# Order of SyncE's transfers, conv2 groups and row-tile waits in a two-stage convolution kernel

## What is computed

```python
x = x + L0(gn(x))      # 3x3 depthwise convolution, then three 32x32 channel mixes
x = x + L1(gn(x))      # deformable 3x3 convolution
# L1, for the normalized input v:
off = conv3x3(v, w_off)                  # 64 channels: a row and a column offset per pixel
r, c = clip(off + grid, 0, 127)
mapped = bilinear sample of v at (r, c)
return conv3x3(mapped, w_conv) + b_conv
```

## Time and profile before

| what | us |
|---|---|
| median of 3 runs | 734.21 (733.68 to 735.55) |
| the profiled execution | 738.19 |
| span of its instructions | 736.3 |
| PE busy | 655.6 (89%) |
| DVE busy | 528.4 (72%) |
| POOL busy | 478.8 (65%) |
| ACT busy | 451.1 (61%) |
| DMA engines, queue of SyncE | 57.6% of 16 engines' time |

### The profile page before, as it was taken

The page is one execution under the profiler, slowest core; times in us unless marked ns, Lnnn a source line. Parts: engine busy times, 40 slices in busy tenths (PEclk is TensorE's granted clock), DMA queues, the critical chain, the costliest instruction groups (busy, mean ns, idle before and its releaser), DMA issues.

```text
span 736.3 us, 16859 instructions
## 1 busy us (share of the span) xinstructions
PE 655.6 (89%) x6572; PEld 297.2 (40%) x6572; DVE 528.4 (72%) x1027; ACT 451.1 (61%) x778; POOL 478.8 (65%) x412
## 2 busy tenths in 40 slices
PE   4799877888996999889997999989997999789965
PEld 4334433344442444434442444433443444344422
DVE  3686987558894688828886488848987386567872
ACT  7236757676754766556665766548656666576740
POOL 4013746969687476857768376876768476977650
PEclk9999999989998999989998999999999999989989
DMA  8958723589348894498747894498945623457555
GB/s 143 186 112 152 117 59 75 137 165 160 75 105 192 176 171 115 120 210 164 141 107 168 179 201 103 106 208 174 154 114 140 145 60 77 106 126 184 128 125 130
DMA packets 135413, 101.40 MB, mean 138 GB/s; under 512 B 13696, under 2 KB 112544, under 8 KB 135328
## 3 DMA queue, kind: packets, MB, share of 16 engines
q1 hardware_dynamic: 111296, 88.47, 57.6%
q10 hardware_dynamic: 24032, 11.78, 9.6%
HBM read 31.59 MB, written 16.78 MB: 66 GB/s over the span
## 4 chain that ended last, share of the span: by engine, by line
PE 39%; SPq 21%; ACT 7%; DVE 6%; issue 5%; POOL 5%; DMA 2%; ACTq 1%; DVEq 0%; POOLq 0%
PE off_ps L816 21%; SPq L429 11%; PE c_ps L698 9%; PE off_ps L698 7%; SPq L500 7%; DMA out_dram<-x1a 2%; DVE other_row L1426 2%; ACT off_abs L1010 2%; SPq L461 1%; ACT down_ps L1008 1%; ACT beyond L1020 1%; ACT other_row L997 1%; SPq L464 1%; DVE xb L1504 1%; POOL other_col L1231 1%
## 5 line engine op out<-in xcount | busy, mean ns | idle before, releaser
L816 PE MATMUL off_ps<-x1a,wo 32*64 32x512 f32 x4608 | 289.2, 611 | 22.6 <-ACT x1a L965 12.4
L816 PEld LDWEIGHTS off_ps<-x1a,wo 32*64 32x64 f32 x4608 | 162.1, 133 | 149.8 <-issue 65.7
L1426 DVE COPY_PREDICATED other_row<-down_ps,row_diff 128x768 f32<-128x768 int32 x128 | 124.6, 1027 | 117.5 <-ACT down_ps L1008 117.5
L997 ACT ACTIVATE other_row<-row_diff 128x768 f32<-128x768 f32 x128 | 101.1, 839 | 57.9 <-POOL row_diff L1207 26.3
L1223 POOL TENSOR_TENSOR other_row<-other_row,x_strips 128x512 f32<-128x512 f32 x48 | 57.2, 1192 | 118.2 <-DVE other_row L1440 118.2
L1224 POOL TENSOR_TENSOR other_col<-other_col,other_row 128x512 f32<-128x512 f32 x64 | 87.8, 1372 | 43.6 <-DVE other_row L1440 43.6
L1008 ACT ACTIVATE down_ps<-off_ps,bias_o 128x512 f32<-128x512 f32 x64 | 42.0, 655 | 100.3 <-PE off_ps L816 85.9
L698 PE MATMUL off_ps<-xb,w 128*64 128x512 f32 x198 | 90.3, 605 | 8.2 <-DVE xb L1504 7.0
L698 PE MATMUL c_ps<-xb,w 128*64 128x512 f32 x138 | 74.5, 682 | 22.0 <-ACT x1a L965 22.0
L700 PE MATMUL off_ps<-xa,w 128*64 128x512 f32 x198 | 90.3, 605 | 0.0
L1231 POOL TENSOR_TENSOR other_col<-other_col,off_abs 128x512 f32<-128x512 f32 x64 | 82.8, 1294 | 5.0
(11 more groups left out here) (160 smaller groups left out, 1059.9 us busy)
## 6 DMA issues: line engine op xcount, KB each, us to landing
mapa<-mapped SPq DMA_DIRECT2D x224, 65.0 KB, 2.1
mapb<-mapa SPq DMA_DIRECT2D x28, 520.0 KB, 6.4
out_dram<-x1a SPq DMA_DIRECT2D x49, 256.0 KB, 4.7
xb<-in_x_dram SPq DMA_DIRECT2D x48, 256.0 KB, 10.6
xa<-in_x_dram ACTq DMA_DIRECT2D x40, 256.0 KB, 7.4
x_strips<-x1a SPq DMA_DIRECT2D x112, 81.2 KB, 2.1
x_strips<-x1a SPq DMA_DIRECT2D x112, 65.0 KB, 2.0
xa<-in_x_dram SPq DMA_DIRECT2D x16, 256.0 KB, 6.5
```

The costliest lines, as they stand in the source:

```text
L816: last = nc.tensor.matmul(tiles[side][64 * t:64 * t + 64, CH * n:CH * n + CH], wo[wpar][Q * r:Q * r + Q, 3 * ky + kx, :], x1a[par][Q * r:Q ...
L997: act.activation(other_row[n][:, :, KR // 2 * odd:KR // 2 * odd + KR // 2, :], diff_of_chunk(k, odd), ACT.Copy)
L1426: last = dve.copy_predicated(other_row[n][:, :, KR // 2 * odd:KR // 2 * odd + KR // 2, :], bass.AP(tensor=rows.tensor, offset=rows.offset ...
```

## The change

Four things change. SyncE moves half 1 of the strips of image i in round i, behind store part 1, and no longer half 1 of the strips of image i + 1 with half 0; accordingly the clamp of half 1 moves behind step 1 on ScalarE, and the row differences of pair 2 behind chunk 2 on GpSimd. The conv2 groups go in the order 0, 2, 1, 3, 4, 6, 5, 7, store part 0 waits for four added groups instead of six and stands ahead of half 0 of mapa, which waits for six groups (four for the spread images). And the offsets have one counter `row_step` with one wait per kernel row, for all that was issued before, with the row groups always in the order 0 to 3.

```diff
--- before.py
+++ after.py
@@ -58,8 +58,9 @@
 
     BANKS = ["", "c", "xc", "xyc", "cxyc", "ycxyc"]
 
-    CONV2_GROUPS = [0, 2, 4, 6, 1, 3, 5, 7]
-    STORE_AFTER = [6, 8]
+    CONV2_GROUPS = [0, 2, 1, 3, 4, 6, 5, 7]
+    STORE_AFTER = [4, 8]
+    HALF_READ = 6
     BEFORE_END_GROUPS = [1, 2, 3, 0, 4, 5, 6, 7]
 
 
@@ -307,7 +308,7 @@
         first2_done = sem("first_group_of_conv2_done")
         x1_ready = sem("x1_ready")
         off_done = [sem(f"off_done_side{n}") for n in range(2)]
-        row_step = [sem(f"row_step_of_rows{n}") for n in range(4)]
+        row_step = sem("row_step")
         off_used = sem("off_used")
         parts_ready = sem("parts_ready")
         cols_ready = sem("cols_ready")
@@ -554,9 +555,6 @@
             for i in range(NB):
                 prev, nxt, after = i >= 1, i + 1 < NB, i + 2 < NB
                 if prev:
-
-                    if i == 1:
-                        move_strips(sp, i, 1)
                     sp.wait_ge(map_pads, i)
                     sp.wait_ge(mapa_moved[0], A_MOVES * DMA * i)
                     copy_mapb(0)
@@ -564,6 +562,7 @@
                     sp.wait_ge(out_ready, 8 * (i - 1))
                     store(sp, i - 2, (i - 2) % 3, 1)
                 if prev:
+                    move_strips(sp, i, 1)
                     sp.wait_ge(mapped_ready, NK * i)
                     if i >= 2:
                         sp.wait_ge(conv2_done, 8 * (i - 1))
@@ -585,8 +584,7 @@
 
                     sp.wait_ge(x1_pads, i + 2)
                     sp.wait_ge(mapped_ready, NK * i + 4)
-                    for half in range(2 if prev else 1):
-                        move_strips(sp, i + 1, half)
+                    move_strips(sp, i + 1, 0)
                 if not nxt:
                     if i >= 2:
                         sp.wait_ge(out_ready, 8 * (i - 1))
@@ -607,14 +605,13 @@
                     for part in range(2):
                         store(sp, i - 1, (i - 1) % 3, part)
                     break
-                if prev:
-                    sp.wait_ge(mapped_ready, NK * i + 4)
-                    sp.wait_ge(conv2_done, 8 * (i - 1) + 4)
-                    sp.wait_ge(mapped_pads, 2 * i + 1)
-                    move_mapa(0)
                 if prev and after:
                     sp.wait_ge(out_ready, 8 * (i - 1) + STORE_AFTER[0])
                     store(sp, i - 1, (i - 1) % 3, 0)
+                if prev:
+                    sp.wait_ge(conv2_done, 8 * (i - 1) + (4 if spread(i - 1) else HALF_READ))
+                    sp.wait_ge(mapped_pads, 2 * i + 1)
+                    move_mapa(0)
 
 
             for m in (1, 3, 5):
@@ -803,14 +800,13 @@
 
                 half, parity = s // 2, s % 2
                 for ky in range(3):
-                    order = [(3 + ky + n) % 4 for n in range(4)]
+                    if ky > 0:
+
+                        pe.wait_ge(row_step, 16 * (NS * i + s) + 8 * ky)
                     for kx in range(3):
-                        for r in order:
+                        for r in range(4):
                             c = (r - ky) % 4
                             side, n, shift = c % 2, c // 2, (c + ky) // 4
-                            if ky > 0 and kx == 0:
-
-                                pe.wait_ge(row_step[(r - 1) % 4], 4 * (NS * i + s) + 2 * ky)
                             for t in range(2):
                                 b = 2 * NJ * t + NJ * half + parity + shift
                                 last = nc.tensor.matmul(tiles[side][64 * t:64 * t + 64, CH * n:CH * n + CH],
@@ -818,7 +814,7 @@
                                                         x1a[par][Q * r:Q * r + Q, b:b + 7:2, kx:kx + W],
                                                         start=(ky == 0 and kx == 0), stop=(ky == 2 and kx == 2))
                                 if kx == 2 and ky < 2:
-                                    last.then_inc(row_step[r], 1)
+                                    last.then_inc(row_step, 1)
                                 elif kx == 2:
                                     last.then_inc(off_done[side], 1)
 
@@ -1091,6 +1087,7 @@
                     sum_far(i, b)
                     if s == 0:
                         pad_mapped(i, i % 3, 0)
+                    if s == 1:
                         clamp(i, 1)
                     if s == 1 and not nxt:
                         pad_end(i % 3)
@@ -1236,8 +1233,8 @@
                         pool.wait_ge(mapa_moved[k // 4], A_MOVES * DMA * i)
                     pool.tensor_tensor(mapped_of_chunk(k), split(side), split(column),
                                        ALU.add).then_inc(mapped_ready, 1)
-                    if k in (1, 3):
-                        row_steps(i, 2 + k // 2)
+                    if k in (2, 3):
+                        row_steps(i, k)
                     elif k >= NK - 2 and i + 1 < NB:
                         row_steps(i + 1, k % 2)
 
```

## The result

The changed kernel took 741.0 us (median of 20 runs, 735.7 to 745.2) against 734.2 us for the kernel before (20 runs on the same chip): 1.0086 of it, 95% interval [1.0061, 1.011]. So it is slower by 0.9%, where the forecast had said 0.9% faster; 741.0 lies outside the range. Its profiled execution took 743.9 us with a span of 742.1.

A forecast was written before the change was run, and what follows sets the result against it. The prediction took PE's work plus its waits as the bound, SyncE's queue almost a second. Store waits -33.2, conv2 waits +15.4, half clock +6, image 1 +2.2, steps +3, end +0.6 gave -6.0; the chain's -6.6 gave 727.7 us, range 714 to 739.

The forecast's parts named there:

- S: Start of the strips on SyncE's queue; forecast at 191.7 in image 1.
- S + 70.8: Landing of the mapb copy that conv2's first group needs: 69.1 us after the strips start, plus 1.7.
- part (b): SyncE's queue: half 0 of mapa waits for six conv2 groups, and its landing is paid again, 1.7 us per round.
- C: Time at which conv2's first group starts on PE; forecast 262.5 in image 2, 592.1 in image 6.
- Rival 2: Slower: the mapb copy falls further behind, through 16 strips, half 1 of mapa and their landings; 735 to 741, chance 0.24.
- (d): Later clamp on ScalarE and row differences on GpSimd: strips 3.1 us later, about 2.2 us of PE in image 1.
- S = A + 13.3: Strips start 10.2 us after PE is free for conv2, as before, plus 3.1 for the later differences.
- A: Time at which PE is free for conv2's first group; forecast 78.7 us after the previous image's C.
- the sixth group: Conv2 group that half 0 of mapa awaits, C + 25; where later than the queue, the copy lands 54.9 after.
- (a): Store part 0 goes 22 us earlier in SyncE's queue, ending the store waits with their low clock: -33.2 us.
- (e): One wait per kernel row: each PE step 8.92 us, +0.1; +3 us over 32 steps, bounds -5 and +12.
- w: Delay between a kernel row's end and seeing its last tile's increment; taken 0.20 us, bounds 0.07 and 0.33.

The follow-up runs named there:

- experiment 6: Kernel before with only the clamp of half 1 one step later and row differences 2 and 3 behind chunks 2 and 3: 752.6 us, 1.0261.
- experiment 5: Changed kernel with the four row-step semaphores and rotated order of before, so both queue moves without the one counter: 737.9 us, 1.0062 of the kernel before.
- experiment 14: Whole change, one counter too, with the clamp between step 1's two chunks and differences behind chunks 1 and 3: 731.2 us, 0.9931 of the kernel before.
- experiment 4: Kernel before with only the new group order and store part 0 ahead of half 0 of mapa, which waits for six groups: 723.2 us, 0.9851.
- experiment 2: Kernel before with its four counters all waited for ahead of each kernel row, row tiles in fixed order: 740.1 us, 1.0100.
- experiment 3: Kernel before with only the strips' half 1 moved one round later, with the later clamp and row differences: 727.0 us, 0.9921.
- experiment 11: Kernel before with the new group order and store part 0 between the two halves of the strips, differences as before, four counters: 724.9 us, 0.9878.

## Why the prediction was wrong

The chain of times in the prediction can be held against the trace point by point. The forecast span was 729.7, the measured one 742.1: 12.4 us to find. They lie in three places: 4.9 us up to the strips of image 1, 3.8 and 2.6 us between the strips and the copy that PE waits for, in images 2 and 4, and 1.1 us behind conv2 of image 6 (forecast 137.6 us, measured 138.7).

- **The step that failed: the copy's lag behind the strips, S + 70.8 in part (b).** C, the start of conv2, was to come 70.8 us after S. Measured: 271.19 - 196.60 = 74.6 in image 2, 439.50 - 366.08 = 73.4 in image 4, and 603.36 - 533.83 = 69.5 in image 6. In image 2 the queue waits 4.8 us for the landing of half 1 of mapa, where the term has the 2.6 us of before in it, and the 16 strip moves take 12.4 us instead of 11.0; in image 4 the copy lands after up to 9.4 us where the earlier trace rows had 7.1. Rival 2 had this as its mechanism and its place, "half 1 of mapa and their landings, right behind store part 1 and beside ScalarE's x loads".
- **Up to the strips of image 1: (d) at the start of the kernel, too small.** S was forecast at 191.7 and is 196.60 in the queue above. Of the 4.9 us, 1.4 were there before anything changed had run. PE's first offsets, before and after:

```profile
54.56 0.68 PE L816 MATMUL off_ps<-x1a,wo 32*64 32x512 f32 x7
```

```profile
55.94 0.69 PE L812 MATMUL off_ps<-x1a,wo 32*64 32x512 f32 x8
```

  In the traces of all runs this start lies between 54.49 and 56.01, so times up to image 1 have to be counted from it. I had costed the late differences at 2.2 us of PE, once, in image 1, and wrote "PE has work meanwhile, save in image 1". Counted from the first offsets, experiment 6 has PE's step 3 late by 1.4 us in image 0 and by 1.9 more in image 1, and the strips of image 1 late by 3.8 us. In image 0 PE was waiting at that place before the change too, and in image 1 there is the 2.0 us wait for VectorE's add that I had seen:

```profile
111.56 0.68 PE L816 MATMUL off_ps<-x1a,wo 32*64 32x512 f32 x6 [2.33 <-ACT x1a L965]
```

```profile
114.09 0.69 PE L816 MATMUL off_ps<-x1a,wo 32*64 32x512 f32 x8 [2.71 <-ACT x1a L965]
...
191.70 3.77 PE L816 MATMUL off_ps<-x1a,wo 32*64 32x512 f32 x56 [2.01 <-DVE x1a L1411]
```

  (The first is the kernel before, the two others experiment 6.) Counted the same way, the changed kernel's strips come 1.3 us later than those of experiment 5, which lacks the one counter; I had 0.4. About 1.0 us between experiments 5 and 6 has no cause that I can name; single traces without any late differences scatter by 2 us here.
- **Later on (d) was priced about right, though the sum doesn't show it.** Its 3.1 us stand in S = A + 13.3 as well. By the prediction's own rules, with A + 10.2 and without the 2.2 us, conv2 of image 6 would start at 581.9 instead of 592.1, with one low clock less behind it: 12 us in all. The runs have 11 (1.0086 against 0.9931 in experiment 14). So the late differences are what turns this change from a gain into a loss, but they are not what the forecast missed: by the same rules experiment 14 should take some 716 us, and 0.9931 is 729.
- **Between the images the agreement is in part luck.** From C to C: forecast 81.9, 82.9, 81.9, 82.9; measured 82.0, 86.3, 81.5, 82.4. The forecast put the first and the third down to the copy, late by the sixth group, with PE waiting 1.2 us. In the trace PE does not wait there (353.22 and 520.97 above): its own round is longer. From C to the next A it is 80.0 us, low clock taken off, where the forecast had 78.7. Steps longer by 0.3 us instead of 0.1 make 0.8 of that, the rest is open. The 86.3 is the 2.6 us of lag, and 0.8 because the strips follow an A that is C itself here. The waits for the copy add up to 16.2 us where 15.4 were forecast, but as three and not five, with a low clock behind each of the three.
- **(a) was right as far as it went.** The waits behind the store went, 22.0 to 3.0 us. Alone, though, this part is worth 11 us (experiment 4), not 33 less the copy's: PE that comes early waits for the copy.
- **(e) was near its upper bound.** w is 0.30 us, bounds 0.07 and 0.33, taken 0.20. The share of the counter in the time is 0.24 to 0.48% (1.8 to 3.5 us) against 3 forecast, though a step grows by 0.3 us and not by 0.1. The estimate by the Trainium skill ("TensorE: Matmul & The Clock Gate", section "The cost: per-tile semaphore tail"), w near 0.23, was nearer than my middle. Whether the increments come one behind another or the array runs empty before the next pass, these runs don't tell; experiment 2 has the same eight increments.
- **Rival 2's time came (735 to 741), with less of its mechanism than it asked for.** It wanted a lag of 92 us from A to the landing. Measured, from A over S to C: 87.6, 86.3 and 82.4 us in images 2, 4 and 6. The late start and PE's longer round did the rest.

Why do two gains become a loss? By the ratios the late differences cost 2.6% alone (19 us), 1.7% beside the early store (13), 1.55% in the whole change (11, from 1.0086 to 0.9931) and 1.85% beside the moved strips (14, from 0.9921 to 0.9736). The early store and the moved strips aim at the same wait: with the clamp between the chunks the moved strips give 2.6% and the two together only 1.0%. Why the early store then even costs 1.7%, 12 us, is not settled. Its trace has the queue standing 8.3 us at half 0 of mapa for the sixth group, which the moved strips alone don't have; a version with the moved strips, the early store and half 0 free after four groups wasn't tried.

## What to carry to other kernels

When a transfer is moved in a queue, look at what was moved on other engines to make room for it: here the moves in the queue gain 1.0%, and row differences and a clamp that went to a place where ScalarE waits for them cost 1.55%. A delay called hidden has to be checked in every image, the first ones too, by the idle time in front of the waiting step. Price the parts of a change together: two parts that remove the same wait were worth less here than either alone (1.0% against 2.6 and 1.5). And hold a chain of times against the trace term by term: two of these rounds came out right by a term that did not act.

## What was not expected of the hardware

The landing of the 16 mapa moves (65 KB each) in image 2 took 1.9 us in experiment 3, where ScalarE's four x loads (256 KB each) were issued from 253.29, behind the last move (250.75), and 5.9 us in experiment 5, where three of the four went out at 253.99 to 255.83, ahead of the last move (256.62). In the changed kernel they overlap as well: 4.8 us. In experiment 11 the loads go out at 249.6 to 253.1, beside the moves that end at 252.94, and the landing takes 5.4 us. So in image 2 the landing came 3 to 4 us later where 1 MB of another engine's queue was issued beside the last of these moves. In image 4 of experiment 5 (loads from 423.2, last move ending at 425.0) it took 3.6 us, so the size isn't fixed; and no run moved the loads alone, so that they are the cause is likely but not shown.
